# A one-core attention and mixture-of-experts kernel: the second layer norm's inverse deviation is applied to logits and gates instead of to the tokens

## Chip, cores and metric

The kernel runs on one core of a Trainium2 chip. The metric is the device time of one execution in microseconds (us), the median over several runs; lower is better. The engines are TensorE (PE), VectorE (DVE), ScalarE (ACT), GpSimd (POOL) and SyncE (SP, which here only issues transfers).

## What is computed

The input x is 4 images of 64 channels and 1024 positions. The reference, cut to its steps:

```
x = x + wo . softmax_j(k_i . q_j) v            # q, k, v: 32 channels, per image
t = tokens of x                                # 1024 tokens of 64 values per image
t = t + softmax(u u^T) u,      u = layernorm(t)
w = layernorm(t)
logits = w @ router_w + router_b               # 8 experts
top-2 of the softmax over the experts, renormalised: gates
t = t + sum over the 2 chosen experts of gate * (w @ expert_w + expert_b)
```

The last block is the one that the change touches. Layer norm is (t - mean) / sqrt(var + eps), one mean and one variance for each token.

## The kernel before

Every engine has an instruction stream written by hand; streams meet only at semaphores (wait_ge on one side, then_inc on the other). Each image b = 0 to 3 passes through the same stages, and the images are staggered, so that PE works on the first attention of one image, the second attention of the image before it, and the experts of the one before that. T = 8 tiles of 128 tokens make an image.

PE writes most results into a ring of three PSUM buffers of 2 x 512 columns. The list ORDER fixes which use of the ring comes when; use n may start only when use n - 3 has been read (`release` names the semaphore that tells it).

The stages of an image that matter here, with their names:

- `tokens2` (DVE): divides the second attention's output by its row sums (odiv, L1210) and adds the tokens (tok2, L1215).
- `stats_of_2` (DVE): eight BN_STATS, six small operations on 128x8 (L1172 to L1179; the last one signals var2_ready), and cen2 = 8 * (t - mean) (L1180).
- `rstd` (POOL): the inverse deviation, sm2[:, 3, :] = (...)^-0.5 (L372).
- `normalize2` (DVE): wn = cen2 * inverse deviation (L1220), which waits for POOL's L372.
- `w_transposed` (PE, L586): four transposes of wn into the ring ("wT"); `round_w` (ACT, L941) copies them to w_hi, `split_w` (DVE, L1225) makes the rest w_lo.
- `route` (PE, L599): the router's product, high and low weights apart ("rt"); `top2` (DVE, L1233 to L1264): the logits, the two largest of them, and the gates. In the middle of it L1243 makes the gap between the two largest logits, and ACT's `gap_exp` (L945) waits for that gap; ACT runs in order, and the exponentials of an attention stand behind it.
- `experts` (PE, L610): products of w_hi and w_lo with the expert weights, two tiles at a time (g = 0 to 3); `weigh_experts` (DVE, L1275) multiplies them by the gates into prod. POOL sums over experts (L384 to L388, and for the last two images L423), and PE adds what is left in the last two images (L640).
- `copy_agg` (ACT, L925) and `project_out` (PE, L536) end the first attention of an image and feed `tokens1` (DVE, L1156 on); `weigh` (PE, L499) is the product with the probabilities, `copy_att2` (ACT, L929) and `att2_transposed` (PE, L578) end the second attention.

In the last stage DVE's order is: weigh_experts(2, 0), tokens2(3), stats_of_2(3), weigh_experts(2, 1), normalize2(3), weigh_experts(2, 2), split_w(3), weigh_experts(2, 3), top2(3), weigh_experts(3, 0 to 3). POOL's L423 on the products of (2, 1), (2, 2), (2, 3) and (3, 0), (3, 1), (3, 2) runs beside it.

Of the kernel before, what the change touches and what calls it, by code (L numbers as in the profile page):

```python
# [17 lines left out]
ALU = mybir.AluOpType  # L18
# [6 lines left out]
P = 128  # L25
B, C, N, M, E = 4, 64, 1024, 32, 8
CHUNK = 512
T = N // P
# [54 lines left out]
def build(nc, x, wq, wk, wv, wo, rw, rb, ew, eb, out):  # L83
    ctx = ExitStack()
    with ctx:
        def sb(name, shape, dt=F32):
            return ctx.enter_context(nc.sbuf_tensor(name, shape, dt))

        def sem(name):
            return ctx.enter_context(nc.semaphore(name))  # L90

        def two(name, shape, dt=F32):
            return [sb(f"{name}_{n}", shape, dt) for n in range(2)]
# [41 lines left out]
        w_hi = two("w_hi", [P, CHUNK], F32R)  # L135
        w_lo = two("w_lo", [P, CHUNK], F32R)
        gate = two("gate", [P, 2 * T, E])
        ob = two("ob", [P, CHUNK])

        rowmax = sb("rowmax", [P, T])  # L140
# [13 lines left out]
        stats2 = sb("stats2", [P, T, 6])  # L154
        sm2 = sb("sm2", [P, 7, T])
        cen2 = sb("cen2", [P, T, C])
        wn = sb("wn", [P, T, C])
        lg_1 = sb("lg_1", [P, T, E])
        lg = sb("lg", [P, T, E])
        top8 = sb("top8", [P, T, E])  # L160
# [77 lines left out]
        s_ve2 = sem("var2_ready")  # L238
        s_cen2 = sem("centered2_ready")
        s_rs2 = sem("rstd2_ready")  # L240
        s_w = sem("w_ready")
        s_wr = sem("w_rounded")
        s_ws = sem("w_split")
        s_lg1 = sem("logits_first_part")
        s_lg = sem("logits_ready")
        s_top = sem("top2_step")
        s_gap = sem("logit_gap_ready")
        s_eg = sem("gap_exp_ready")
        s_gate = sem("gates_ready")
        s_gT = sem("gates_turned")  # L250
        s_gt = sem("gates_transposed")
        s_gb = sem("expert_bias_summed")
# [21 lines left out]
        def filled(engine, name, b):  # L274
            buf, n = PLACE[(name, b)]
            engine.wait_ge(s_fill, n + 1)
            return ring[:, buf]
# [60 lines left out]
        def _(pool):  # L338
# [77 lines left out]
            rstd(2, s_ve2, s_rs2, sm2)  # L416
            rstd(3, s_ve2, s_rs2, sm2)

            pool.wait_ge(s_w, B)
            for b, pairs in ((2, (1, 2, 3)), (3, (0, 1, 2))):  # L420
                for n, g in enumerate(pairs):
                    pool.wait_ge(s_prod, (T // 2) * b + g + 1)
# [5 lines left out]
        def _(pe):  # L428
            taken = iter(range(len(ORDER)))

            def take(name, b):
                buf, n = PLACE[(name, b)]
                assert n == next(taken), (name, b)
                if n >= RING:
                    pe.wait_ge(*release(*ORDER[n - RING]))
                return ring[:, buf]
# [143 lines left out]

            def w_transposed(b):
                buf = take("wT", b)
                pe.wait_ge(s_w, b + 1)
                w_flat = wn[:, :, :].rearrange("p t c -> p (t c)")
                for g in range(T // 2):
                    mm = pe.transpose(buf[:, 0, g * P:(g + 1) * P], w_flat[:, g * P:(g + 1) * P], ident[:, :])  # L586
                mm.then_inc(s_fill, 1)
# [62 lines left out]
            buf = take("w3", 0)  # L650
# [109 lines left out]
            weigh_pair1(2, 2)  # L760
            scores1(2, 5)
            w_transposed(0)
            scores1(2, 6)
            weigh_pair1(2, 4)
# [40 lines left out]
            weigh_pair1(3, 2)  # L805
            scores1(3, 5)
            w_transposed(1)
            scores1(3, 6)
            weigh_pair1(3, 4)
# [35 lines left out]
            weigh_pair2(3, 2)  # L845
            scores2(3, 5)
            w_transposed(2)
            scores2(3, 6)
            weigh_pair2(3, 4)
# [270 lines left out]
        def _(dve):  # L1120
            def wide(a, n):

                return a.unsqueeze(2).to_broadcast([P, T, n])
# [11 lines left out]
            def row_max(b, tile):  # L1135
                dve.tensor_reduce(rowmax[:, tile:tile + 1], flat(filled(dve, f"mx{tile}", b)), AX.X, ALU.max).then_inc(s_mx, 1)  # L1136
# [49 lines left out]
            def stats_of_2(b):  # L1186
                norm_stats(tok2[b % 2], s_tk2, stats2, sm2, cen2, s_ln2, s_ve2, s_cen2, b)
# [26 lines left out]
                    dve.wait_ge(s_y, b - 1)  # L1214
                dve.tensor_tensor(tok2[b % 2][:, :, :], odiv[:, :, :], tok1[b % 2][:, :, :], ALU.add).then_inc(s_tk2, 1)  # L1215

            def normalize2(b):
                dve.wait_ge(s_cen2, b + 1)
                dve.wait_ge(s_rs2, b + 1)
                dve.tensor_tensor(wn[:, :, :], cen2[:, :, :], wide(sm2[:, 3, :], C), ALU.mult).then_inc(s_w, 1)  # L1220

            def split_w(b):
                buf, _ = PLACE[("wT", b)]
                dve.wait_ge(s_wr, b + 1)
                dve.tensor_tensor(w_lo[b % 2][:, :], ring[:, buf, 0, :], w_hi[b % 2][:, :].bitcast(F32),  # L1225
                                  ALU.subtract).then_inc(s_ws, 1)

            def top2(b):

                buf = filled(dve, "rt", b)  # L1230
                own = gate[b % 2]
                parts = buf[:, 0, 0:2 * T * E].rearrange("p (t a e) -> p t a e", a=2, e=E)
                dve.tensor_tensor(lg_1[:, :, :], parts[:, :, 0, :],  # L1233
                                  rb_all[:, :].unsqueeze(1).to_broadcast([P, T, E]), ALU.add).then_inc(s_lg1, 1)
                dve.wait_ge(s_lg1, b + 1)
                dve.tensor_tensor(lg[:, :, :], parts[:, :, 1, :], lg_1[:, :, :], ALU.add).then_inc(s_lg, 1)
                dve.wait_ge(s_lg, b + 1)
                top = Steps(dve, s_top, 9, b)
                dve.tensor_copy(landing[:, :], lg[:, 0, 0:1])
                for tile in range(T):  # L1240
                    last = dve.max(top8[:, tile, :], lg[:, tile, :])
                top.then(last)
                dve.tensor_tensor(gm[:, 2, :], top8[:, :, 1], top8[:, :, 0], ALU.subtract).then_inc(s_gap, 1)  # L1243

                both = lg[:, :, :].unsqueeze(1).to_broadcast([P, 2, T, E])
                top.then(dve.tensor_tensor(cand[:, :, :, :], both, top8[:, :, 0:2].rearrange("p t n -> p n t").unsqueeze(3)
                                           .to_broadcast([P, 2, T, E]), ALU.is_equal))
                top.then(dve.tensor_tensor(cand[:, :, :, :], cand[:, :, :, :],
                                           ramp[:, :, :].unsqueeze(1).to_broadcast([P, 2, T, E]), ALU.mult))
                top.then(dve.tensor_reduce(gm[:, 0, :], cand[:, 0, :, :], AX.X, ALU.max))  # L1250
                top.then(dve.tensor_tensor(pick1[:, :, :], cand[:, 0, :, :], wide(gm[:, 0, :], E), ALU.is_equal))

                dve.scalar_tensor_tensor(out=cand2[:, :, :], in0=pick1[:, :, :], scalar=-2.0 * E, in1=cand[:, 1, :, :],
                                         op0=ALU.mult, op1=ALU.add)
                dve.wait_ge(s_eg, b + 1)
                top.then(dve.tensor_scalar(gm[:, 4, :], gm[:, 3, :], 1.0, None, ALU.add))
                dve.tensor_reduce(gm[:, 1, :], cand2[:, :, :], AX.X, ALU.max)
                top.then(dve.reciprocal(gm[:, 5, :], gm[:, 4, :]))
                dve.tensor_tensor(pick2[:, :, :], cand2[:, :, :], wide(gm[:, 1, :], E), ALU.is_equal)
                top.then(dve.tensor_tensor(gm[:, 6, :], gm[:, 3, :], gm[:, 5, :], ALU.mult))  # L1260
                dve.tensor_tensor(pick2[:, :, :], pick2[:, :, :], wide(gm[:, 6, :], E), ALU.mult)
                top.then(dve.tensor_tensor(pick1[:, :, :], pick1[:, :, :], wide(gm[:, 5, :], E), ALU.mult))
                top.end()
                dve.tensor_tensor(own[:, 0:T, :], pick1[:, :, :], pick2[:, :, :], ALU.add).then_inc(s_gate, 1)  # L1264

            def weigh_experts(b, g):
                buf = filled(dve, f"e{g}", b)
                if g == 0:
                    dve.wait_ge(s_gate, b + 1)
                if b in (1, 2):  # L1270
                    dve.wait_ge(s_half, (T // 2) * (b - 1) + g + 1)
                if b == 3:
                    dve.wait_ge(s_sums, g + 1)
                gates = gate[b % 2][:, 2 * g:2 * g + 2, :].unsqueeze(3).to_broadcast([P, 2, E, C])
                dve.tensor_tensor(prod[:, g].rearrange("p e h c -> p h e c"), buf.rearrange("p h (e c) -> p h e c", c=C),  # L1275
                                  gates, ALU.mult).then_inc(s_prod, 1)

# [12 lines left out]
            buf = filled(dve, "w3", 0)  # L1290
# [72 lines left out]
            row_max(3, 2)  # L1363
            stats_of_2(0)
            row_max(3, 3)
            normalize2(0)
            split_w(0)
            row_max(3, 4)
            top2(0)
# [14 lines left out]

            tokens2(1)
            stats_of_2(1)
            normalize2(1)
            split_w(1)
            top2(1)

# [8 lines left out]

            tokens2(2)  # L1400
            stats_of_2(2)
            normalize2(2)
            split_w(2)
            top2(2)

# [3 lines left out]
            tokens2(3)  # L1409
            stats_of_2(3)  # L1410
            weigh_experts(2, 1)
            normalize2(3)
            weigh_experts(2, 2)
            split_w(3)
            weigh_experts(2, 3)
# [3 lines left out]
            g = T // 2 - 1  # L1419
# [28 lines left out]
```

## Time and profile before

| | |
|---|---|
| median of 3 runs | 206.97 us (206.75 to 207.73) |
| profiled execution: its own time, its span | 206.87 us, 204.8 us |
| PE busy | 190.6 us (93% of the span) |
| DVE busy | 142.6 us (70%) |
| ACT busy | 108.1 us (53%) |
| POOL busy | 62.9 us (31%) |
| granted TensorE clock | full in all of the span |

Times in the trace count from the start of the span. "Idle before" is how long an engine stood still in front of an instruction, with what ended it. The span is 2.07 us shorter than the time of the same execution, which also has what lies before the first and behind the last recorded instruction.

### The profile page before, as it was taken

How to read it: one execution, taken by the hardware profiler on the slowest of the kernel's cores; microseconds unless marked ns; L12 is line 12 of the kernel's file. 1: busy time of each engine (PE TensorE's matmuls, PEld its weight loads, DVE VectorE, ACT ScalarE, POOL GpSimd, SP SyncE). 2: the span in 40 equal slices, each digit the busy share in tenths (PEclk: the TensorE clock that was granted, in tenths of full speed). 3: DMA queues.
4: the chain of work that ended last, by engine and by line, in shares of the span. 5: the costliest groups of instructions: out<-in, count | busy, mean ns of one | idle time of the engine just before them, and what ended most of it. 6: DMA issues, size and time to landing. Idle time of an engine off the chain costs nothing.

```text
span 204.8 us, 2988 instructions
## 1 busy us (share of the span) xinstructions
PE 190.6 (93%) x1093; PEld 96.8 (47%) x1093; DVE 142.6 (70%) x359; ACT 108.1 (53%) x172; POOL 62.9 (31%) x79
## 2 busy tenths in 40 slices
PE   7989999999999899998989999799999999798993
PEld 2668644464434334543443544253444324386782
DVE  2889666778747894694588865628795361998990
ACT  3765845458845466564376556466563865301010
POOL 8384000003000300012003479700369860026170
PEclk9999999999999999999999999999999999999999
DMA  3890000000000000000000000010000001000022
GB/s 114 200 165 0 3 0 0 2 2 3 0 0 0 3 0 0 0 0 3 0 2 0 3 2 0 18 34 0 3 0 0 3 11 42 0 3 0 0 54 51
DMA packets 3502, 3.69 MB, mean 18 GB/s; under 512 B 2208, under 2 KB 2464, under 8 KB 3488
## 3 DMA queue, kind: packets, MB, share of 16 engines
q1 hardware_dynamic: 3248, 3.45, 7.5%
q8 instruction: 9, 0.15, 0.3%
q10 hardware_dynamic: 240, 0.05, 0.1%
q14 instruction: 5, 0.04, 0.1%
HBM read 2.45 MB, written 1.05 MB: 17 GB/s over the span
## 4 chain that ended last, share of the span: by engine, by line
PE 63%; DVE 23%; POOL 6%; issue 3%; ACT 2%; DMA 1%; SPq 0%; DVEq 0%; POOLq 0%
PE acc L499 20%; PE ring L563 9%; PE ring L474 6%; DVE rowmax L1136 6%; PE ring L492 6%; PE ring L610 3%; POOL sm L372 3%; PE acc L640 2%; PE ring L536 2%; DVE prod L1275 2%; PE ring L547 2%; PE ring L483 2%; DVE stats L1169 2%; PE ring L447 2%; DMA xin<-in_x 1%
## 5 line engine op out<-in xcount | busy, mean ns | idle before, releaser
L372 POOL TENSOR_TENSOR sm<-sm,minus_half 128x8 f32<-128x8 f32 x8 | 15.8, 1974 | 115.8 <-DVE sm L1179 115.8
L920 ACT ACTIVATE prob<-ring,shift 128x1024 f32<-128x1024 f32 x32 | 35.5, 1111 | 23.7 <-PE ring L563 23.3
L1136 DVE TENSOR_REDUCE rowmax<-ring 128x1 f32<-128x1024 f32 x32 | 38.0, 1219 | 12.5 <-PE ring L474 12.4
L917 ACT ACTIVATE prob<-ring 128x1024 f32<-128x1024 f32 x32 | 32.0, 1023 | 19.6 <-PE ring L492 19.5
L499 PE MATMUL acc<-prob,u 128*64 128x512 f32 x128 | 31.2, 606 | 0.4 <-ACT prob L920 0.4
L499 PE MATMUL acc<-prob,val 128*64 128x512 f32 x128 | 31.0, 605 | 0.0
L474 PE MATMUL ring<-qst,kst 96*128 96x512 f32 x64 | 21.9, 429 | 1.2 <-DVE rowmax L1136 0.8
L1275 DVE TENSOR_TENSOR prod<-ring,gate 128x1024 f32<-128x1024 f32 x16 | 19.3, 1220 | 5.1 <-PE ring L610 4.0
L492 PE MATMUL ring<-kst,qst 98*128 98x512 f32 x64 | 21.1, 422 | 0.4 <-DVE rowmax L1136 0.4
L563 PE MATMUL ring<-zsw,zst 64*128 64x512 f16 x64 | 19.4, 376 | 0.0
L563 PE MATMUL ring<-zst,zsw 64*128 64x512 f16 x64 | 19.2, 376 | 0.0
L492 PEld LDWEIGHTS ring<-kst,qst 98*128 98x128 f32 x64 | 10.5, 188 | 11.1 <-ACT prob L917 5.9
L499 PEld LDWEIGHTS acc<-prob,u 128*64 128x64 f32 x128 | 7.7, 136 | 15.9 <-issue 12.5
L499 PEld LDWEIGHTS acc<-prob,val 128*64 128x64 f32 x128 | 7.7, 136 | 15.2 <-issue 12.4
L474 PEld LDWEIGHTS ring<-qst,kst 96*128 96x128 f32 x64 | 10.1, 189 | 9.7 <-DVE rowmax L1136 3.3
L563 PE MATMUL ring<-zst 64*128 64x512 f16 x32 | 12.3, 386 | 0.7 <-DVE rowmax L1136 0.4
L384 POOL TENSOR_TENSOR half<-prod 128x512 f32<-128x512 f32 x8 | 10.6, 1319 | 7.1 <-DVE prod L1275 6.9
L610 PE MATMUL ring<-e,w_hi 64*128 64x512 f32 x64 | 12.4, 443 | 0.0
L563 PE MATMUL ring<-zsw 64*128 64x512 f16 x32 | 12.4, 386 | 0.0
L423 POOL TENSOR_TENSOR prod<-prod 128x512 f32<-128x512 f32 x6 | 7.5, 1279 | 5.8 <-DVE prod L1275 4.9
L563 PEld LDWEIGHTS ring<-zst 64*128 64x128 f16 x32 | 3.0, 93 | 13.3 <-issue 6.5
L1169 DVE BATCH_NORM_STATS2 stats<-tok 128x6 f32<-128x64 f32 x64 | 8.9, 211 | 0.2
(160 smaller groups left out, 319.7 us busy)
## 6 DMA issues: line engine op xcount, KB each, us to landing
xin<-in_x SPq DMA_DIRECT2D x6, 256.0 KB, 5.0
out<-ob SPq DMA_DIRECT2D x6, 128.0 KB, 2.3
xin<-in_x SPq DMA_DIRECT2D x4, 128.0 KB, 2.8
e_in<-in_L_ffn_expert_w SPq DMA_DIRECT2D x2, 128.0 KB
out<-ob SPq DMA_DIRECT2D x4, 64.0 KB, 2.0
eb_in<-in_L_ffn_expert_b SPq DMA_DIRECT2D x8, 2.0 KB
wo<-in_L_conv_wo SPq DMA_DIRECT2D x2, 8.0 KB, 2.2
r_in<-in_L_ffn_router_w SPq DMA_DIRECT2D x2, 2.0 KB
```

The costliest lines, as they stand in the source:

```text
L372: pool.tensor_tensor(sm[:, 3, :], sm[:, 2, :], minus_half[:, :], ALU.pow).then_inc(s_rs, 1)
L384: pool.tensor_tensor(half[:, :, :, :], p[:, 0:E // 2], p[:, E // 2:E], ALU.add).then_inc(s_half, 1)
L474: mm = pe.matmul(buf[:, h, :], kst[home][0:ROW, col(tile):col(tile) + P], qst[home][0:ROW, h * CHUNK:(h + 1) * CHUNK], start=True, stop=True)
L492: mm = pe.matmul(buf[:, h, :], qst[home][0:ROW + 2, col(j):col(j) + P], kst[home][0:ROW + 2, h * CHUNK:(h + 1) * CHUNK], start=True, stop= ...
L499: mm = pe.matmul(acc[h * C:(h + 1) * C, :], stationary[:, j, :], prob[:, j % DEEP, h * CHUNK:(h + 1) * CHUNK], start=(j == 0), stop=(j == ...
L563: mm = pe.matmul(buf[:, h, :], held[h][rows, col(j):col(j) + P], moving[h][rows, h * CHUNK:(h + 1) * CHUNK], start=(n == 0), stop=(n == 2))
L610: mm = pe.matmul(buf[:, h, :], w[rows, g * P:(g + 1) * P], e[rows, :], start=(n == 0), stop=(n == 2))
L917: act.activation(prob1[:, j % DEEP, :], flat(filled(act, f"st{j}", b)), ACT.Exp).then_inc(s_p1, 1)
L920: act.activation(prob2[:, j % DEEP, :], flat(filled(act, f"s{j}", b)), ACT.Exp, bias=shift[:, :], accum_out=rsum2[b % 2][:, j:j + 1]).then ...
L1136: dve.tensor_reduce(rowmax[:, tile:tile + 1], flat(filled(dve, f"mx{tile}", b)), AX.X, ALU.max).then_inc(s_mx, 1)
L1169: last = dve.bn_stats(stats[:, tile, :], tok[:, tile, :])
L1275: dve.tensor_tensor(prod[:, g].rearrange("p e h c -> p h e c"), buf.rearrange("p h (e c) -> p h e c", c=C), gates, ALU.mult).then_inc(s_pr ...
```

## The change

The tokens are no longer multiplied by the inverse deviation. The centred tokens cen2 go through the transposes, the split, the router and the experts; the router's two partial products are multiplied by the inverse deviation when they leave PSUM (lg_2, 128x128, a new instruction, which is also the one that frees the ring buffer "rt"), and a copy of the gates times the inverse deviation (gate_r, 128x64, a new instruction) weighs the experts. The unscaled gates still go to the expert biases.

```
-                dve.tensor_tensor(wn[:, :, :], cen2[:, :, :], wide(sm2[:, 3, :], C), ALU.mult).then_inc(s_w, 1)
...
-            pool.wait_ge(s_w, B)
+            pool.wait_ge(s_cen2, B)
...
-                pe.wait_ge(s_w, b + 1)
-                w_flat = wn[:, :, :].rearrange("p t c -> p (t c)")
+                pe.wait_ge(s_cen2, b + 1)
+                w_flat = cen2[:, :, :].rearrange("p t c -> p (t c)")
...
-                parts = buf[:, 0, 0:2 * T * E].rearrange("p (t a e) -> p t a e", a=2, e=E)
-                dve.tensor_tensor(lg_1[:, :, :], parts[:, :, 0, :],
+                dve.wait_ge(s_rs2, b + 1)
+                dve.tensor_tensor(lg_2[:, :, :, :].rearrange("p t a e -> p t (a e)"),
+                                  buf[:, 0, 0:2 * T * E].rearrange("p (t n) -> p t n", t=T),
+                                  wide(sm2[:, 3, :], 2 * E), ALU.mult).then_inc(s_lg, 1)
+                dve.wait_ge(s_lg, b + 1)
+                dve.tensor_tensor(lg_1[:, :, :], lg_2[:, :, 0, :],
                                   rb_all[:, :].unsqueeze(1).to_broadcast([P, T, E]), ALU.add).then_inc(s_lg1, 1)
-                dve.wait_ge(s_lg1, b + 1)
-                dve.tensor_tensor(lg[:, :, :], parts[:, :, 1, :], lg_1[:, :, :], ALU.add).then_inc(s_lg, 1)
-                dve.wait_ge(s_lg, b + 1)
+                dve.wait_ge(s_lg1, 2 * b + 1)
+                dve.tensor_tensor(lg[:, :, :], lg_2[:, :, 1, :], lg_1[:, :, :], ALU.add).then_inc(s_lg1, 1)
+                dve.wait_ge(s_lg1, 2 * b + 2)
...
                 dve.tensor_tensor(own[:, 0:T, :], pick1[:, :, :], pick2[:, :, :], ALU.add).then_inc(s_gate, 1)
+                dve.wait_ge(s_gate, b + 1)
+                dve.tensor_tensor(gate_r[b % 2][:, :, :], own[:, 0:T, :], wide(sm2[:, 3, :], E), ALU.mult).then_inc(s_gr, 1)
...
                 if g == 0:
-                    dve.wait_ge(s_gate, b + 1)
+                    dve.wait_ge(s_gr, b + 1)
```

Three places show what moves. The first is DVE in the last stage, from the centring of image 3 to the start of its top2; before, it reads:

```order
L1180 SCALAR_TENSOR_TENSOR cen<-tok_1,sm 128x512
L1275 TENSOR_TENSOR prod<-ring,gate 128x2x8x64 [waits prods_used,ring_filled]
L1220 TENSOR_TENSOR wn<-cen,sm 128x512 [waits rstd2_ready,centered2_ready]
L1275 TENSOR_TENSOR prod<-ring,gate 128x2x8x64 [waits prods_used,ring_filled]
L1225 TENSOR_TENSOR w_lo<-ring,w_hi 128x512 [waits w_rounded]
L1275 TENSOR_TENSOR prod<-ring,gate 128x2x8x64 [waits prods_used,ring_filled]
L1233 TENSOR_TENSOR lg<-ring,rb_all 128x64 [waits ring_filled]
L1236 TENSOR_TENSOR lg<-ring,lg 128x64 [waits logits_first_part]
L1239 COPY landing<-lg 128x1 [waits logits_ready]
```

The same place of the changed kernel (its lines are numbered one to four apart from those of before):

```order
L1181 SCALAR_TENSOR_TENSOR cen<-tok_1,sm 128x512
L1277 TENSOR_TENSOR prod<-ring,gate_r 128x2x8x64 [waits prods_used,ring_filled] x2
L1221 TENSOR_TENSOR w_lo<-ring,w_hi 128x512 [waits w_rounded]
L1277 TENSOR_TENSOR prod<-ring,gate_r 128x2x8x64 [waits prods_used,ring_filled]
L1229 TENSOR_TENSOR lg<-ring,sm 128x128 [waits rstd2_ready,ring_filled]
L1233 TENSOR_TENSOR lg<-lg,rb_all 128x64 [waits logits_scaled]
L1236 TENSOR_TENSOR lg<-lg 128x64 [waits logits_step]
L1239 COPY landing<-lg 128x1 [waits logits_step]
```

The wait for POOL's inverse deviation has moved from behind the first product to the start of top2, wn is gone, and the first addition to the logits (L1233) now reads lg_2 in SBUF where it read the ring in PSUM.

The second place is PE in the same stage, where the transposes of image 3 follow the sums over the experts of image 2; before, and then in the changed kernel:

```order
L633 MATMUL acc<-gate_t,eb_blk 128x128 x4
L640 MATMUL acc<-ident,prod 128x128 [waits prods_ready]
L640 MATMUL acc<-ident,prod 128x128 x7
L586 MATMUL ring<-ident,wn 128x128 [waits w_ready,prods_ready]
L586 MATMUL ring<-ident,wn 128x128 x3
L610 MATMUL ring<-e,w_hi 128x512 [waits prods_ready]
```

```order
L634 MATMUL acc<-gate_t,eb_blk 128x128 x4
L641 MATMUL acc<-ident,prod 128x128 [waits prods_ready]
L641 MATMUL acc<-ident,prod 128x128 x7
L587 MATMUL ring<-ident,cen 128x128 [waits centered2_ready,prods_ready]
L587 MATMUL ring<-ident,cen 128x128 x3
L611 MATMUL ring<-e,w_hi 128x512 [waits prods_ready]
```

No PE instruction moves; the transposes wait for the centred tokens instead of the scaled ones, in all four images.

The third place is the end of DVE's top2(2), in the changed kernel:

```order
L1261 TENSOR_TENSOR pick<-pick,gm 128x64 [waits top2_step]
L1262 TENSOR_TENSOR pick<-pick,gm 128x64
L1264 TENSOR_TENSOR gate<-pick 128x64 [waits top2_step]
L1266 TENSOR_TENSOR gate_r<-gate,sm 128x64 [waits gates_ready]
L1406 RECIPROCAL rinv<-rsum_1 128x8 [waits probs2_ready]
L1277 TENSOR_TENSOR prod<-ring,gate_r 128x2x8x64 [waits prods_used,gates_scaled,ring_filled]
```

One instruction, gate_r, has come between the gates and the products; before, the reciprocal (L1407) followed the gates (L1264) directly.

## Rows read from the trace of the kernel before

**Rows 1.** The chain that ended last, share of the span by engine.
```profile
PE 63%; DVE 23%; POOL 6%; issue 3%; ACT 2%; DMA 1%; SPq 0%; DVEq 0%; POOLq 0%
```

**Rows 2.** Waits: engine, line, releaser: us in total, times, longest.
```profile
ACT gm L945 <- DVE gm L1243: 10.3, 4, 3.3
```

**Rows 3.** Timeline of PE, images 0 and 1: start, us, instructions [idle before <-releaser].
```profile
92.78 0.73 PE L492 MATMUL ring<-kst,qst 98*128 98x512 f32 x2
94.15 0.63 PE L586 MATMUL ring<-ident,wn 128*128 128x128 f32 x4 [0.64 <-DVE wn L1220]
...
133.16 0.73 PE L492 MATMUL ring<-kst,qst 98*128 98x512 f32 x2
133.77 0.63 PE L586 MATMUL ring<-ident,wn 128*128 128x128 f32 x4
```

**Rows 4.** Timeline of ACT, PE and DVE around the gap of image 0.
```profile
101.78 0.21 ACT L945 ACTIVATE gm<-gm 128x8 f32<-128x8 f32 x1 [2.94 <-DVE gm L1243]
103.71 0.46 PE L536 MATMUL ring<-wo_blk,agg 128*128 128x130 f32 x2 [0.53 <-ACT agg L925]
104.88 0.21 DVE L1156 RECIPROCAL rinv<-ring 128x8 f32<-128x8 f32 x1 [0.40 <-PE ring L536]
```

**Rows 5.** Timeline of ACT and PE behind the gap of image 1.
```profile
140.90 0.58 ACT L925 ACTIVATE agg<-acc 128x512 f32<-128x512 f32 x1
141.63 1.13 PE L536 MATMUL ring<-wo_blk,agg 128*128 128x130 f32 x8
```

**Rows 6.** Timeline of PE behind the gap of image 2.
```profile
176.86 1.08 PE L499 MATMUL acc<-prob,u 128*64 128x512 f32 x4 [0.40 <-ACT prob L920]
178.63 0.66 PE L578 MATMUL acc<-ident,att 128*128 128x128 f32 x4 [0.70 <-ACT att L929]
```

**Rows 7.** Timeline of DVE, top2 of image 2: small operations.
```profile
174.04 0.22 DVE L1233 TENSOR_TENSOR lg<-ring,rb_all 128x64 f32<-128x64 f32 x1 [1.78 <-PE ring L599]
174.30 0.22 DVE L1236 TENSOR_TENSOR lg<-ring,lg 128x64 f32<-128x64 f32 x1
...
175.39 0.28 DVE L1246 TENSOR_TENSOR cand<-lg,top 128x128 f32<-128x128 f32 x1
```

**Rows 8.** Timeline of all engines, last stage: single rows of it.
```profile
182.76 0.69 DVE L1180 SCALAR_TENSOR_TENSOR cen<-tok,sm 128x512 f32<-128x512 f32 x1
185.89 0.63 PE L586 MATMUL ring<-ident,wn 128*128 128x128 f32 x4 [0.73 <-DVE wn L1220]
187.18 0.69 DVE L1225 TENSOR_TENSOR w_lo<-ring,w_hi 128x512 fp32r<-128x512 f32 x1 [0.31 <-ACT w_hi L941]
187.79 1.21 DVE L1275 TENSOR_TENSOR prod<-ring,gate 128x1024 f32<-128x1024 f32 x1
185.87 2.51 POOL L423 TENSOR_TENSOR prod<-prod 128x512 f32<-128x512 f32 x2 [0.93 <-DVE wn L1220]
189.08 1.29 POOL L423 TENSOR_TENSOR prod<-prod 128x512 f32<-128x512 f32 x1 [0.70 <-DVE prod L1275]
189.17 0.22 DVE L1236 TENSOR_TENSOR lg<-ring,lg 128x64 f32<-128x64 f32 x1
190.16 0.23 DVE L1243 TENSOR_TENSOR gm<-top 128x8 f32<-128x8 f32 x1
194.51 0.73 PE L610 MATMUL ring<-e,w_hi 64*128 64x512 f32 x4
```

**Rows 9.** Timeline, DVE and POOL at once, images 1 and 2.
```profile
128.85 1.28 POOL L397 TENSOR_TENSOR y<-yres,ybias 128x512 f32<-128x512 f32 x1
128.91 1.24 DVE L1173 SCALAR_TENSOR_TENSOR sm<-stats 128x8 f32<-128x8 f32 x1
...
163.30 0.69 DVE L1215 TENSOR_TENSOR tok<-odiv,tok 128x512 f32<-128x512 f32 x1
163.38 1.74 POOL L397 TENSOR_TENSOR y<-yres,ybias 128x512 f32<-128x512 f32 x1
...
165.26 0.17 DVE L1173 SCALAR_TENSOR_TENSOR sm<-stats 128x8 f32<-128x8 f32 x1
```

More of the change, by code:

```diff
@@ L137, in build @@
         gate = two("gate", [P, 2 * T, E])
+        gate_r = two("gate_r", [P, T, E])
         ob = two("ob", [P, CHUNK])
@@ L156, in build @@
         cen2 = sb("cen2", [P, T, C])
-        wn = sb("wn", [P, T, C])
+        lg_2 = sb("lg_2", [P, T, 2, E])
         lg_1 = sb("lg_1", [P, T, E])
@@ L240, in build @@
         s_rs2 = sem("rstd2_ready")
-        s_w = sem("w_ready")
         s_wr = sem("w_rounded")
         s_ws = sem("w_split")
-        s_lg1 = sem("logits_first_part")
-        s_lg = sem("logits_ready")
+        s_lg = sem("logits_scaled")
+        s_lg1 = sem("logits_step")
         s_top = sem("top2_step")
@@ L249, in build @@
         s_gate = sem("gates_ready")
+        s_gr = sem("gates_scaled")
         s_gT = sem("gates_turned")
@@ L1215, in tokens2 @@
                 dve.tensor_tensor(tok2[b % 2][:, :, :], odiv[:, :, :], tok1[b % 2][:, :, :], ALU.add).then_inc(s_tk2, 1)
-            def normalize2(b):
-                dve.wait_ge(s_cen2, b + 1)
-                dve.wait_ge(s_rs2, b + 1)
-                dve.tensor_tensor(wn[:, :, :], cen2[:, :, :], wide(sm2[:, 3, :], C), ALU.mult).then_inc(s_w, 1)
             def split_w(b):
@@ L1273, in weigh_experts @@
                     dve.wait_ge(s_sums, g + 1)
-                gates = gate[b % 2][:, 2 * g:2 * g + 2, :].unsqueeze(3).to_broadcast([P, 2, E, C])
+                gates = gate_r[b % 2][:, 2 * g:2 * g + 2, :].unsqueeze(3).to_broadcast([P, 2, E, C])
                 dve.tensor_tensor(prod[:, g].rearrange("p e h c -> p h e c"), buf.rearrange("p h (e c) -> p h e c", c=C),
@@ L1365, in _ @@
             row_max(3, 3)
-            normalize2(0)
             split_w(0)
@@ L1386, in _ @@
             stats_of_2(1)
-            normalize2(1)
             split_w(1)
@@ L1401, in _ @@
             stats_of_2(2)
-            normalize2(2)
             split_w(2)
@@ L1411, in _ @@
             weigh_experts(2, 1)
-            normalize2(3)
             weigh_experts(2, 2)
```

## The prediction, written before the changed kernel ran

> **What bounds the kernel now.** The first view is the chain that ended last, by engine: PE holds 63% of the span, DVE 23%, POOL 6% [rows 1]. So a DVE instruction counts only where the chain leaves PE. The view of waits shows where that may be. ACT stands 10.3 us in all in front of `gap_exp`, once per image, for DVE's gap of the logits [rows 2]. The timeline then has three kinds of place. At the transposes of wn, PE stands still 0.64 us in image 0 and 0.73 us in image 3, both times for wn, which itself has waited for POOL's inverse deviation; in image 1 the transposes follow without a stop [rows 3, 8], and in image 2 too. Behind the gap of image 0 ACT goes on with an exponential and the copy agg, and PE waits 0.53 us for agg [rows 4]; in image 1 agg ends at 140.90 + 0.58 = 141.48 and PE's L536 starts at 141.63, just behind it [rows 5]; in image 2 PE waits 0.40 and 0.70 us for ACT [rows 6]. Last, from the third product of image 2 to the last stage's end, DVE's top2(3) leads: the experts' product of (3, 3) on PE starts at 194.51, when DVE's first product of image 3 has freed the ring [rows 8].
>
> **The change, part by part.** *New lg_2.* It is 128x128, PSUM times SBUF. The nearest rows: 0.22 us for 128x64 from PSUM, 0.28 for 128x128 from SBUF, and a dependent instruction starts 0.26 after the one of 0.22 [rows 7]. I take 0.28 and a step of 0.32 us; bounds 0.26 (no cost for the second 64 columns) and 0.35. It stands before the gap, so every gap is 0.32 later than it would be. *New gate_r.* 128x64, 0.22 us, a step of 0.26. It stands behind the gap; in images 0 and 1 DVE then waits for PE anyway (0.40 us before L1156 in image 0 [rows 4]), and in image 2 the PE path below covers it. In image 3 nothing hides it. *Gone: wn*, 0.69 us on DVE, and the wait for POOL in front of it.
>
> *Image 0.* PE no longer waits. In image 1, with no wait, the transposes start 133.77 - 133.16 = 0.61 us behind the product before them; here 94.15 - 92.78 = 1.37. The difference is 0.76, a little more than the idle time shown, since loading the first weights also hides. cen2 has been ready since before L492 here. Copy w_hi, w_lo, route and the next maximum follow 0.75 earlier, the gap 0.75 - 0.32 = 0.43 earlier, and agg, L536 and everything behind them as well: **-0.43 us** (-0.32 if only the idle time of 0.64 is saved).
>
> *Image 1.* No wait for wn to save, and the gap comes 0.32 later. agg is what PE waits for, with nothing to spare: **+0.32 us**. It goes on into tokens1(3), which waits for L536.
>
> *Image 2.* The gap is 0.32 later, so the last exponential, PE's L499 at 176.86 and the transposes at 178.63 are: +0.32 on PE. DVE is 0.58 later (lg_2 and gate_r) when it comes to tokens2(3), so cen2 of image 3 ends at 182.76 + 0.69 + 0.58 = 184.03. PE would be free for the transposes at about 185.16 + 0.32 = 185.48 (185.89 less the idle 0.73, later by the gap), so PE sets their start, not DVE. They start 0.73 - 0.32 = 0.41 us earlier than before by the idle time alone, and 0.52 if the first weights hide as in image 0 (0.11 more). I take **-0.52** for them, and so for w_hi, w_lo and the product of (2, 3), which wait for each other in a row. POOL's inverse deviation was there before the transposes of wn at 185.89; 0.58 later it is still in time for top2(3), which starts behind the product of (2, 3) at 187.79 [rows 8].
>
> *Top2(3).* Here an addition changes its kind. L1233 read PSUM and SBUF; now it reads lg_2 and rb_all, both in SBUF, while POOL's L423 works on the product of (2, 3). Rows 9 show what that means: DVE's L1173 on 8 columns, both inputs in SBUF, takes 0.17 us at 165.26 with POOL idle, and 1.24 at 128.91, begun 0.06 after POOL's L397, ending at 130.15 where POOL ends at 130.13. The other way round, DVE's L1215 began 0.08 before L397, took its usual 0.69, and POOL's took 1.74 instead of 1.28 [rows 9]. An operation with one input in PSUM is not held: L1225 takes 0.69 in the middle of two L423 [rows 8]. L1243 at 190.16 (both inputs in SBUF) ends at 190.39, POOL's L423 at 190.37 [rows 8]. So who comes first holds the other off until it ends. Before, POOL starts 189.08 - 187.79 = 1.29 us behind the start of the product, and L1236 at 1.38. The new L1233 stands where L1236 stood plus the 64 columns of lg_2, at 1.45, which is 0.16 after POOL; POOL ends at 2.58. The addition ends at about 2.65 (64 columns at 1.05 ns, from L1225's 0.69 for 512 against 0.22 for 64), not at 1.67: **+0.98 us**, bounds 0 (it comes first) and 1.2 (it comes right behind and runs in full). Against that, L1243 isn't held any more: 0.23 against the 0.17 of such an operation, -0.06. With lg_2 0.32 and gate_r 0.26, top2(3) gives +0.98 - 0.06 + 0.58 = +1.50, less the 0.52 saved: **+0.98** at the first product of image 3. PE waits for that product, and POOL, DVE and PE keep their distances to the end.
>
> The Trainium skill, "SBUF — State Buffer", the section on the single rule of port contention, says that a VectorE instruction with two SBUF inputs and a GpSimd instruction that reads SBUF exclude each other for a whole instruction, and that the issue order decides who blocks. By that rule the trace agrees, at each place named; by a model without it the sum would be near -0.1.
>
> *The sum:* -0.43 + 0.32 + 0.98 = +0.87 against the profiled execution's 206.87, which stands 0.10 under the median of 206.97; the difference is laid on the median: 207.8. Savings by idle time alone and a late hold give +1.1; the longest hidden weights and a step of 0.26 for lg_2 give +0.6. So 207.5 to 208.1 if the addition is held.
>
> **The rivals.** *The addition isn't held.* It needs POOL to start 0.16 us later, or DVE earlier. For it: the lead of 0.16 is small, and worked out from three durations. Against: 0.06 was enough at 128.91 [rows 9]. Then the sum is -0.43 + 0.32 + 0.58 - 0.06 - 0.52 = -0.11: 206.9.
>
> *Faster: ACT's wait for the gap has slack.* If exponentials behind `gap_exp` were not on the path, lg_2 would cost nothing in images 1 and 2, and image 0 would keep its 0.75. Then 206.97 - 0.75 - 0.84 (0.52 + 0.32 at the transposes of image 3) + 0.52 (top2(3), not held) = 205.9; with the hold 206.9. It decides from 0.32 us of slack between agg and L536. The rows speak against it: in all three images PE waits for ACT or starts 0.15 behind it [rows 4, 5, 6].
>
> *More slower: image 0's gain doesn't arrive.* Something else than wn (the exponential that frees the ring, w_hi queued behind an exponential on ACT) would hold the route. Then 0.75 comes on top: 207.84 + 0.75 = 208.6. Against it: in image 1 the transposes had nothing to wait for, and PE has no idle time before its route or the product behind it.
>
> *The change doesn't act.* PE's order is the same, only the semaphore differs, and the centring really ends before PE is free in images 0 and 3; this one I leave at nothing.
>
> **Chances.** Held addition, as forecast: 0.67. Not held: 0.15. Slack at the gap: 0.06. Gain lost: 0.12. A measurement of this kernel tells about 0.5%, 1.03 us, from no change. The forecast's sum is 0.4%, with about a quarter of its weight above 0.5%: slower 0.17 + 0.12 + 0.03 = 0.32; faster 0.06; same 0.62. The range takes in the not held case below and most of the lost gain above: 206.7 to 208.5.
>
> **What would show it.** Held: in the changed profile the addition to lg_2 in image 3 takes about 1.2 us and ends where L423 on the product of (2, 3) ends, and 0.22 in images 0 to 2. PE's idle time before the transposes of cen2 is gone in images 0 and 3, there 0.41 to 0.52 us earlier against L578 of the second attention moved by 0.32. The distance from the transposes to L536 in image 0 is 0.32 longer, in image 1 L536 has an idle time of about 0.3 for agg. The prediction is wrong if the hold is missing, if L536 in image 1 isn't later against y's transposes, or if the time of the tail behind the first product of image 3 changes.

## The result and the profile after

| | before | after |
|---|---|---|
| median of 20 runs | 206.94 us | 207.68 us |
| span of the profiled execution | 204.8 us | 205.4 us |
| PE, DVE, ACT, POOL busy | 190.6, 142.6, 108.1, 62.9 us | 190.1, 142.9, 108.0, 62.9 us |

The ratio is 1.003, with a 95% interval of 1.0021 to 1.0038: the change costs 0.3%, some 0.6 to 0.7 us, clear of the noise and under the 0.5% that the prediction took as the least difference to be told. The forecast was 207.8. One of the 20 runs of the kernel before (215.15 us) and five of the 20 of the changed kernel (210.6 to 210.9 us, at a mean granted clock of 0.984) fell in a slower state, and such runs are left out of this ratio and all below.

The chain that ended last, share of the span by engine; it is [rows 1] with three points of DVE gone and two more on ACT:

```profile
PE 64%; DVE 20%; POOL 6%; ACT 4%; issue 3%; DMA 1%; SPq 0%; DVEq 0%; POOLq 0%
```

The view of waits has the same row as [rows 2], larger by 2.3 us:

```profile
ACT gm L946 <- DVE gm L1243: 12.6, 4, 4.5
```

Image 0 and image 1 in the timeline of PE and ACT of the changed kernel (start, us, instructions, [idle before <-releaser]):

```profile
92.70 0.73 PE L493 MATMUL ring<-kst,qst 98*128 98x512 f32 x2
93.26 0.60 PE L587 MATMUL ring<-ident,cen 128*128 128x128 f32 x4
...
101.18 0.21 ACT L946 ACTIVATE gm<-gm 128x8 f32<-128x8 f32 x1 [3.27 <-DVE gm L1243]
103.12 1.13 PE L537 MATMUL ring<-wo_blk,agg 128*128 128x130 f32 x8 [0.86 <-ACT agg L926]
...
139.38 0.21 ACT L946 ACTIVATE gm<-gm 128x8 f32<-128x8 f32 x1 [1.57 <-DVE gm L1243]
141.31 1.13 PE L537 MATMUL ring<-wo_blk,agg 128*128 128x130 f32 x8 [0.39 <-ACT agg L926]
```

Against [rows 3] the transposes of image 0 follow the product before them after 0.56 us instead of 1.37. Against [rows 4] the gap and L537 (L536 before) come 0.60 and 0.59 earlier, and PE's wait for agg has grown from 0.53 to 0.86: of what PE gained, 0.33 is given back at the gap. Against [rows 5] L537 of image 1 is only 0.32 earlier, with a wait of 0.39 that wasn't there. (All of this execution runs 0.09 us earlier from the first row maximum on, before any changed instruction; that 0.09 is not the change's.)

Behind the gap of image 2, against [rows 6], the same once more, 0.40 grown to 0.73:

```profile
176.90 1.08 PE L500 MATMUL acc<-prob,u 128*64 128x512 f32 x4 [0.73 <-ACT prob L921]
178.68 0.66 PE L579 MATMUL acc<-ident,att 128*128 128x128 f32 x4 [0.70 <-ACT att L930]
```

The last stage, DVE, POOL and PE, against [rows 8]:

```profile
185.02 0.60 PE L587 MATMUL ring<-ident,cen 128*128 128x128 f32 x4
186.29 0.69 DVE L1221 TENSOR_TENSOR w_lo<-ring,w_hi 128x512 fp32r<-128x512 f32 x1 [0.28 <-ACT w_hi L942]
186.90 1.21 DVE L1277 TENSOR_TENSOR prod<-ring,gate_r 128x1024 f32<-128x1024 f32 x1
188.03 0.28 DVE L1229 TENSOR_TENSOR lg<-ring,sm 128x128 f32<-128x128 f32 x1
188.19 1.29 POOL L424 TENSOR_TENSOR prod<-prod 128x512 f32<-128x512 f32 x1 [0.36 <-DVE prod L1277]
188.34 1.21 DVE L1233 TENSOR_TENSOR lg<-lg,rb_all 128x64 f32<-128x64 f32 x1
189.59 0.23 DVE L1236 TENSOR_TENSOR lg<-lg 128x64 f32<-128x64 f32 x1
190.59 0.17 DVE L1243 TENSOR_TENSOR gm<-top 128x8 f32<-128x8 f32 x1
...
193.65 0.30 PE L620 MATMUL acc<-ident,gate 128*128 128x128 f32 x1 [1.72 <-DVE gate L1264]
193.85 2.36 DVE L1277 TENSOR_TENSOR prod<-ring,gate_r 128x1024 f32<-128x1024 f32 x2
195.13 0.73 PE L611 MATMUL ring<-e,w_hi 64*128 64x512 f32 x4 [0.29 <-DVE prod L1277]
```

The first product of image 3 (DVE), where the account below ends, in the kernel before:

```profile
193.23 3.49 DVE L1275 TENSOR_TENSOR prod<-ring,gate 128x1024 f32<-128x1024 f32 x3
```

Up to the product at 186.90 DVE is 0.89 earlier than before (187.79). L1233, an addition over 64 columns, then takes 1.21 us; it begins 0.15 behind POOL's L424 and ends at 189.55, 0.07 behind POOL's end at 189.48. In images 0 to 2, where POOL does nothing meanwhile, the same instruction takes 0.22 to 0.23. DVE's first product of image 3 starts at 193.85 instead of 193.23, and PE's L611 behind it at 195.13 instead of 194.51: the lead of 0.89 has become a lag of 0.62.

### The profile page after: what moved, and what is told of

It reads as the page before. It is cut to its first block, busy times and chain, and to the rows that moved or that the text cites. A ratio compares the mean times of both kernels' runs of the same rounds, so it can differ in the third digit from the quotient of the medians.

```text
span 205.4 us, 2992 instructions
## 1 busy us (share of the span) xinstructions
PE 190.1 (93%) x1093; PEld 96.9 (47%) x1093; DVE 142.9 (70%) x363; ACT 108.0 (53%) x172; POOL 62.9 (31%) x79
## 4 chain that ended last, share of the span: by engine, by line
PE 64%; DVE 20%; POOL 6%; ACT 4%; issue 3%; DMA 1%; SPq 0%; DVEq 0%; POOLq 0%
PE acc L500 21%; PE ring L564 8%; PE ring L493 7%; PE ring L475 6%; DVE rowmax L1137 5%; PE ring L611 3%; PE acc L641 3%; PE ring L537 2%; DVE prod L1277 2%; PE ring L548 2%; POOL half L385 2%; ACT prob L921 2%; PE ring L448 1%; DMA xin<-in_x 1%; PE acc L465 1%
## 5 line engine op out<-in xcount | busy, mean ns | idle before, releaser
L1277 DVE TENSOR_TENSOR prod<-ring,gate_r 128x1024 f32<-128x1024 f32 x16 | 19.2, 1220 | 5.1 <-PE ring L611 4.0
L611 PE MATMUL ring<-e,w_hi 64*128 64x512 f32 x64 | 12.4, 443 | 0.3 <-DVE prod L1277 0.3
L1221 DVE TENSOR_TENSOR w_lo<-ring,w_hi 128x512 fp32r<-128x512 f32 x4 | 2.8, 692 | 11.7 <-ACT w_hi L942 11.7
L424 POOL TENSOR_TENSOR prod<-prod 128x512 f32<-128x512 f32 x6 | 7.5, 1275 | 6.1 <-DVE prod L1277 6.0
```

What stands on the lines that cost most here:

```text
L424: pool.tensor_tensor(prod[:, g, 0:E // 2], prod[:, g, 0:E // 2], prod[:, g, E // 2:E], ALU.add).then_inc(s_half, 1)
L611: mm = pe.matmul(buf[:, h, :], w[rows, g * P:(g + 1) * P], e[rows, :], start=(n == 0), stop=(n == 2))
```

## The experiments

The theory is that of the prediction: four terms, of which the largest is a hold of 1 us on one addition, because DVE's instruction with two inputs in SBUF and POOL's sum exclude each other. Its rivals: two more instructions on DVE are enough to explain the tail; the gap is not what PE waits for; the gain of image 0 is lost later. Ratios stand against runs of the kernel before on the same chip, with 95% intervals. Each edit moves the line numbers by a few; the operands say which instruction it is. Several kernels are compared below on one distance, which leaves out all that happened earlier: from PE's transposes of the second attention of image 3 (L578 of the kernel before) to DVE's first product of image 3.

### lg_2 written to PSUM

```
-                dve.tensor_tensor(lg_2[:, :, :, :].rearrange("p t a e -> p t (a e)"),
-                                  buf[:, 0, 0:2 * T * E].rearrange("p (t n) -> p t n", t=T),
+                scaled = buf[:, 0, 0:2 * T * E].rearrange("p (t n) -> p t n", t=T)
+                dve.tensor_tensor(scaled, scaled,
                                   wide(sm2[:, 3, :], 2 * E), ALU.mult).then_inc(s_lg, 1)
...
-                     "wT": (s_ws, b + 1), "rt": (s_lg, b + 1), "yT": (s_ob, b + 1)}
+                     "wT": (s_ws, b + 1), "rt": (s_lg1, 2 * b + 2), "yT": (s_ob, b + 1)}
```

> The changed kernel with lg_2 written back in place into the ring buffer in PSUM instead of into SBUF, so that both additions to the logits read one operand from PSUM again; the ring buffer is freed by the second addition. Theory (the addition is held off by the sum on POOL): L1233 of image 3 takes 0.22 us instead of 1.21, nothing else moves, and the time falls by 1.0 us from 207.7 to 206.7, 0.2 to 0.4 under the kernel before. Rival (the tail is longer because of the two more DVE instructions, and the long addition is only where DVE waits for something else): 207.6, with the idle time somewhere else in top2(3).

Measured: 206.60 us, ratio 0.9983 (0.9974 to 0.9993). DVE and POOL in its last stage:

```profile
188.27 1.30 POOL L423 TENSOR_TENSOR prod<-prod 128x512 f32<-128x512 f32 x1 [0.37 <-DVE prod L1277]
...
188.11 0.29 DVE L1230 TENSOR_TENSOR ring<-ring,sm 128x128 f32<-128x128 f32 x1
188.44 0.22 DVE L1233 TENSOR_TENSOR lg<-ring,rb_all 128x64 f32<-128x64 f32 x1
188.69 0.22 DVE L1236 TENSOR_TENSOR lg<-ring,lg 128x64 f32<-128x64 f32 x1
```

The same addition begins 0.17 behind the same POOL operation, with one input in PSUM, and is not held. The instructions on DVE are as many as in the changed kernel, so their number does not explain this 1 us. The distance is 192.96 - 178.75 = 14.21 us, against 193.85 - 178.68 = 15.17 in the changed kernel: the hold costs 0.96.

### POOL's sum made short

```
+                    rows = slice(0, 1) if (b, g) == (2, 3) else slice(0, E // 2)
+                    other = slice(E // 2, E // 2 + 1) if (b, g) == (2, 3) else slice(E // 2, E)
+                    cols = slice(0, 8) if (b, g) == (2, 3) else slice(0, C)
-                    pool.tensor_tensor(prod[:, g, 0:E // 2], prod[:, g, 0:E // 2], prod[:, g, E // 2:E],
+                    pool.tensor_tensor(prod[:, g, rows, :, cols], prod[:, g, rows, :, cols], prod[:, g, other, :, cols],
```

> The changed kernel with DVE untouched, but POOL's sum on the product of (2, 3) cut from 128x512 to 128x16, so it leaves out most of that sum. Theory: the POOL operation is over, or nearly, when L1233 of image 3 comes; that addition takes 0.22 to 0.35 us, and the time falls by 0.85 to 1.0 us, to 206.7 to 206.9. Rival (POOL is not the cause): L1233 still takes 1.2 us and the time stays at 207.6.

Measured: 206.49 us, ratio 0.9977 (0.9967 to 0.9988), 0.2 under the lowest that was expected. DVE's program is that of the changed kernel word for word, and the addition is short:

```profile
188.15 0.22 POOL L427 TENSOR_TENSOR prod<-prod 128x16 f32<-128x16 f32 x1 [0.36 <-DVE prod L1280]
...
188.30 0.23 DVE L1236 TENSOR_TENSOR lg<-lg,rb_all 128x64 f32<-128x64 f32 x1
```

POOL's part in it is shown from the other side: 192.82 - 178.63 = 14.19 us on the same distance, so the hold costs 0.98 by this kernel.

### POOL's sum started later

```
+                    if (b, g) == (2, 3):
+                        pool.wait_ge(s_lg1, 2 * B - 1)
```

> The changed kernel with POOL's sum on the product of (2, 3) waiting also for the first addition to the logits of image 3. Theory (who comes first holds the other off, each time anew): L1233 takes 0.22, L1236 comes first as well or is held from its first moment, and if it comes first then POOL starts behind it at about 188.83 and ends at about 190.1, where L1243 (both inputs in SBUF, due at 189.59) ends too: a hold of about 0.5 instead of 1.0, time 207.2. If POOL comes before L1236 the whole hold of 1.2 lies on L1236 instead and the time stays at 207.7. Rival (a hold only ever falls on the first addition): 206.7.

Measured: 206.87 us, ratio 0.9991 (0.998 to 1.0002), lower than the 207.2 of the theory and nearer to the rival's 206.7, so the time alone doesn't decide. The timeline does:

```profile
188.38 0.23 DVE L1235 TENSOR_TENSOR lg<-lg,rb_all 128x64 f32<-128x64 f32 x1
188.64 0.23 DVE L1238 TENSOR_TENSOR lg<-lg 128x64 f32<-128x64 f32 x1
188.75 1.30 POOL L426 TENSOR_TENSOR prod<-prod 128x512 f32<-128x512 f32 x1 [0.88 <-DVE lg L1235]
...
189.64 0.43 DVE L1245 TENSOR_TENSOR gm<-top 128x8 f32<-128x8 f32 x1
190.00 0.28 DVE L1248 TENSOR_TENSOR cand<-lg,top 128x128 f32<-128x128 f32 x1
```

The hold moves on, as the theory says: both additions are free, and the next instruction with two inputs in SBUF, the gap, takes 0.43 instead of 0.17 and ends at 190.07, POOL's sum at 190.05. Its cost is 14.45 us on the distance above, less the 14.20 of the two kernels without a hold: 0.25, not 0.5. The expectation counted the hold from the start of the gap; unheld, the gap would have ended at 189.64 + 0.17 = 189.81, and it ended 0.26 after that. POOL began at 188.75, inside the second addition, and took its usual 1.30 (more on this in the last section).

### lg_2 alone, on the kernel before

```
+                dve.tensor_tensor(lg_2[:, :, :, :].rearrange("p t a e -> p t (a e)"),
+                                  buf[:, 0, 0:2 * T * E].rearrange("p (t n) -> p t n", t=T),
+                                  wide(unit[:, :], 2 * E), ALU.mult).then_inc(s_lg2, 1)
+                dve.wait_ge(s_lg2, b + 1)
-                dve.tensor_tensor(lg_1[:, :, :], parts[:, :, 0, :],
+                dve.tensor_tensor(lg_1[:, :, :], lg_2[:, :, 0, :],
```

> The kernel before with lg_2 alone: the router's products are multiplied by a tile of ones on their way from PSUM to SBUF; wn stays, the gates stay. Theory: +0.33 at the gap of image 0, +0.33 at that of image 1, +0.32 on DVE's way through top2(2) to the centring of image 3, and in top2(3) 0.32 plus a hold of 1.0 less 0.06: +2.2 us in all, 209.15. Rival without a hold: +1.3 us, 208.2. Rival in which the gap has slack: +1.5 us, from top2(2) and top2(3) alone, 208.5.

Measured: 209.20 us, ratio 1.0103 (1.0087 to 1.0119), +2.2. The addition of image 3 takes 1.22 us here too. The start of L536 in image 0 is 0.33 later than before (104.04 against 103.71), in image 1 it is 142.32 against 141.63, another 0.36.

### gate_r alone, on the kernel before

```
+                dve.wait_ge(s_gate, b + 1)
+                dve.tensor_tensor(gate_r[b % 2][:, :, :], own[:, 0:T, :], wide(unit[:, :], E), ALU.mult).then_inc(s_gr, 1)
```

> The kernel before with gate_r alone: the gates are multiplied by a tile of ones into a copy, and the copy weighs the experts. Theory: hidden in images 0 and 1, where DVE then waits for L536; 0.26 in image 2, because before the change DVE and POOL, not PE, set the start of image 3's transposes; 0.26 in image 3: +0.52, 207.45. Rival (hidden in image 2 as well): 207.2. Rival (on the path in all four): 208.0.

Measured: 207.41 us, ratio 1.0027 (1.0015 to 1.0038), +0.56. PE's L536 in images 0 and 1 and the transposes of the second attention of image 3 (178.66, 178.63 before) are where they were; the w transposes of image 3 are 0.28 later (186.17), the first product of image 3 is 0.55 later (193.78). In the changed kernel the first 0.28 is hidden: there PE has no idle time before these transposes, so PE and not DVE sets their start.

### The change in image 0 alone, and in image 3 alone

In both, an image that goes the old way has wn again and neither lg_2 nor gate_r:

```
+                if b in OLD:
+                    pe.wait_ge(s_w, OLD.index(b) + 1)
+                else:
+                    pe.wait_ge(s_cen2, b + 1)
+                w_flat = (wn if b in OLD else cen2)[:, :, :].rearrange("p t c -> p (t c)")
```

> The change in image 0 alone; images 1 to 3 go the old way. Theory: the 0.5 us by which L536 of image 0 came earlier in the changed kernel stay to the end, nothing else differs: 206.4. Rival (the start of image 0's gain is lost again by image 1, and the saving comes from image 3): 206.9.

Measured: 206.51 us, ratio 0.9977 (0.9965 to 0.9989), -0.48. L541 (the L536 of before) of image 0 starts at 103.07, 0.64 earlier than before, and what is behind it keeps this to within 0.03: the first product of image 3 is at 192.62, against 193.23. Of the 0.61 that are left, 0.11 lie before the change's first instruction. The gain of image 0 arrives at the end.

> The change in image 3 alone, with lg_2 in SBUF as in the changed kernel (the ring buffer is freed by the second addition); images 0 to 2 go the old way. Theory: the transposes start 0.9 earlier, top2(3) takes 1.5 more with the hold: +0.57, 207.5. Rival (the saving at the transposes and the cost of the hold cancel): 206.9.

Measured: 207.40 us, ratio 1.0026 (1.0016 to 1.0036), +0.54. The gain and the hold in one view:

```profile
186.91 1.22 DVE L1293 TENSOR_TENSOR prod<-ring,gate 128x1024 f32<-128x1024 f32 x1
...
188.20 1.28 POOL L428 TENSOR_TENSOR prod<-prod 128x512 f32<-128x512 f32 x1 [0.63 <-DVE prod L1293]
188.36 1.21 DVE L1248 TENSOR_TENSOR lg<-lg,rb_all 128x64 f32<-128x64 f32 x1
```

The product is 0.88 earlier than before; the first product of image 3, at 193.86, is 0.63 later. (Here the second addition frees the ring buffer, so PE waits 0.62 us for it at 189.88; that costs nothing at the first product of image 3, which starts 15.18 us behind the transposes at 178.68, against 15.17 in the changed kernel.)

### The change in images 0 and 3, lg_2 in PSUM

OLD is (1, 2) here, and lg_2 stays in the ring as in the first experiment.

> lg_2 in PSUM as in the first experiment, and the change made only in images 0 and 3, where the transposes waited for wn; images 1 and 2 go the old way (wn, no lg_2, no gate_r). Theory: image 0 keeps its gain of 0.5, images 1 and 2 lose nothing (the gap comes 0.33 earlier than in the first experiment in both), image 3 has the 0.92 of the transposes less 0.58 for lg_2 and gate_r and nothing held: 0.95 under the kernel before, 206.0. Rival (the 0.33 of the gap is hidden in images 1 and 2): as the first experiment, 206.6.

The same kernel once more, for its profile:

> The kernel of the old way in images 1 and 2 once more, for a profile of an undisturbed execution. Theory: the gap of image 1 comes 9.4 us behind the transposes of y (9.4 before the change, 9.7 with it), L536 of image 1 follows its predecessor without idle time, image 2 likewise; 206.0 to 206.2.

Measured: 206.24 and then 205.96 us, ratios 0.9962 (0.9948 to 0.9975) and 0.9954 (0.9941 to 0.9966). The gap of image 1 comes 139.22 - 129.80 = 9.42 us behind the transposes of y, and L540 of image 1 has no idle time before it; both as expected. It is 0.2 to 0.3% under the first experiment, which differs only in images 1 and 2: lg_2 costs there, and there is little or nothing to gain.

### The exponential of the gap later in ACT's order

```
-            gap_exp(0)
...
             exp2(1, 0)
             copy_agg(2)
+            gap_exp(0)
```

and so in images 1 and 2 (there it comes behind the last exponential). First on the kernel with the old way in images 1 and 2:

> The kernel of the old way in images 1 and 2, and ACT's order changed: the exponential of the gap comes behind the exponential and the copy agg (images 0 and 1) and behind the last exponential (image 2), so that neither waits for DVE's gap. Theory (PE waits at L536 and at the last L499 only because ACT waits for the gap): L536 of image 0 follows without idle time, of which the next work on DVE lets 0.65 through; 0.13 in image 1; 0.6 in image 2 at w_lo of image 3; together 1.4 less than without it: 204.6 (204.3 to 205.0). Rival (DVE's top2 sets the pace by itself): less than 0.3 gained, 205.8.

Measured: 205.22 us, ratio 0.9919 (0.9906 to 0.9933), the lowest of all, but above the range expected (204.3 to 205.0): it gained 0.7 to 1.0 us of the 1.4. Then with the change in all four images and lg_2 in PSUM:

> The first experiment (the change in all images, lg_2 in PSUM) with ACT's exponential of the gap behind the exponential and the copy agg. If the gap costs its 0.33 in images 1 and 2 only because ACT waits for it, this comes within 0.3 us of the kernel that has the same order of ACT and the old way in those images (205.2): 205.3 to 205.6. If the gap's lateness costs on DVE too, 205.9 or more.

Measured: 205.64 us, ratio 0.9937 (0.9924 to 0.9951), just above what was expected. PE's waits in this kernel between the w transposes of image 0 and those of image 3, without one of 0.18:

```profile
106.94 0.39 PE L563 MATMUL ring<-zst 64*128 64x512 f16 x1 [0.71 <-DVE rowmax L1134]
129.47 0.63 PE L572 MATMUL ring<-ident,y 128*128 128x128 f32 x4 [1.26 <-POOL y L397]
151.68 1.05 PE L547 MATMUL ring<-ident_h,uhl 128*128 128x128 f16 x16 [0.54 <-DVE uhl L1195]
177.20 0.66 PE L578 MATMUL acc<-ident,att 128*128 128x128 f32 x4 [0.70 <-ACT att L929]
```

The last three are in the changed kernel too (1.28, 0.49 and 0.70). The waits for agg (0.86 and 0.39) and for the last exponential (0.73) are gone, so they were the gap's. A new one of 0.71 has come in image 0, for a row maximum that stands behind top2 on DVE; the kernel of 205.22 has it too. It shows why that kernel missed its range. Without the new order its L540 of image 0 (the L536 of before) starts 103.24 - 86.01 = 17.23 us behind the second attention's transposes before it, with it 102.28 - 86.07 = 16.21, so 1.02 is won; at the next transposes of that kind only 0.23 of it are left (38.70 against 38.93 behind the same ones), where 0.65 was expected. In image 1 nothing was won, where 0.13 was expected, and image 2 gave 0.63, as expected.

Last, that order of ACT on the kernel before:

> The kernel before with that order of ACT alone. Theory: 0.6 in image 0 and 0.13 in image 1; nothing in image 2, where DVE and POOL set the start of image 3's transposes: 206.2. Rival (DVE's top2 sets the pace by itself): 206.9.

Measured: 206.53 us, ratio 0.9999 (0.9978 to 1.0021); no difference is shown. Its ten runs fall apart by the granted clock: six at 0.997 or more take 206.25 to 206.57 us (their median is 206.36, not far above the 206.2 expected), three at 0.991 take 207.1 to 207.3, and one at 0.983 takes 208.62. The profiled execution is one of those at 0.991. In it the last stage reaches the transposes 0.55 earlier than before, and then this (view of windows: us, busy time and instructions of PE, PEld, DVE, ACT, POOL, granted clock, share of the DMA engines, GB/s):

```profile
183.00:185.30 2.30, 0.98 (x9) 0.79 (x8) 1.84 (x3) 0.00 (x0) 1.40 (x1) 1.00 0.00 0
...
186.50:188.00 1.50, 1.50 (x12) 1.14 (x8) 1.36 (x2) 0.10 (x1) 1.34 (x2) 0.86 0.00 0
188.00:190.00 2.00, 2.00 (x10) 1.64 (x11) 1.90 (x14) 0.12 (x1) 1.28 (x1) 0.50 0.00 0
190.00:191.00 1.00, 1.00 (x8) 0.73 (x6) 0.86 (x5) 0.09 (x1) 0.00 (x0) 0.50 0.00 0
```

The granted clock is at the lower of its two levels, 1.2 GHz, from about 187.6 (0.86 is the mean over a stretch of 1.5 us) to 191, and the end comes 0.2 later than before. So the order of ACT seems to gain some 0.5 us, and the lower clock takes it back in four runs of ten; the 17 runs of the kernel before beside them have no clock under 0.997. This split was made after the runs, and what makes the clock fall was not tried.

## Why the prediction was right

Term by term, in us, each measured in the profiled execution of the changed kernel against that of before. A place's shift is the difference of its two start times; a term is how far the shift changes from one place to the next.

| term | forecast | shift at its end | measured |
|---|---|---|---|
| before the change's first instruction | 0 | -0.09 | -0.09 |
| image 0: transposes without wait, gap later | -0.43 | -0.59 (L537) | -0.50 |
| image 1: gap later | +0.32 | -0.32 (L537) | +0.27 |
| up to route of image 2 | 0 | -0.29 | +0.03 |
| image 2: gap later | +0.32 | +0.05 (L579) | +0.34 |
| transposes of image 3 against L579, to the product of (2, 3) | -0.84 | -0.89 (DVE L1277) | -0.94 |
| top2(3): hold, lg_2, gate_r | +1.50 | +0.62 (L1277) | +1.51 |
| sum | +0.87 | | +0.62, or +0.71 without the first row |

Behind the first product of image 3 nothing changes, as the forecast said: the span ends 11.57 us after it before, and 11.55 after. The forecast was right by its terms and not by errors that cancel: leaving out the first row, three terms missed by 0.05 to 0.10, all towards a faster kernel, and the others by 0.03 or less.

**The hold.** The forecast was 0.98, and it cost 0.96 or 0.98 (first and second experiment), with the place, POOL's lead (0.16 forecast, 0.15 in the profile) and the end as forecast. Four kernels show its cause: it goes when the addition reads PSUM, it goes when POOL's sum is short, it moves to the gap when POOL comes later, and it appears on the kernel before when lg_2 is put in SBUF. The Trainium skill's "SBUF — State Buffer", under "Who interferes with whom", names this case, two SBUF inputs against a GpSimd instruction that reads SBUF. Its rule that the issue order decides who blocks agrees with the changed kernel, where POOL was first and DVE held for 0.99 us, and with DVE's side of the third experiment, where DVE was first and not held. The three rivals that the forecast priced are out: the addition is held; lg_2 alone cost 0.33 and 0.36 in images 0 and 1, so the gap has no slack; and with the change in image 0 alone its gain of 0.50 is there at the end.

**lg_2 and gate_r.** 0.28 us and a step of 0.32; 0.22 and a step of 0.26, as taken from the rows. gate_r was hidden in images 0 and 1 and, in the changed kernel, in image 2.

**Image 0 and the transposes of image 3.** Both gains were sized from PE's idle time, with 0.11 added for weights that load under the product before. They were 0.50 instead of 0.43 and 0.94 instead of 0.84, so the term that was mis-sized is this one, by 0.07 and 0.10. The row that the first was measured by, image 1 in [rows 3], was itself not free of wn: without wn the transposes follow the product before them after 0.56 or 0.57 us instead of 0.61, and the product behind them after 0.35 instead of 0.39. The whole gain of image 0 at that product is 0.83 (0.91 earlier, at 93.62 against 94.53, less 0.08 from before), where the forecast had 0.75.

**Image 1.** +0.27 instead of +0.32, for the same reason: the product before the transposes is 0.57 earlier than before, the one behind them 0.65 (133.51 against 134.16). The profile of before showed no idle time there, but wn ended at 132.93 + 0.69 = 133.62 and the transposes started 0.15 later. That is the distance at which they follow wn in image 0 too, where PE did wait for it (93.31 + 0.69 = 94.00, then 94.15). The forecast had put the saving of image 1 at nothing; it was 0.08, and the gap then cost its 0.33.

What the whole comes to: PE gains 0.83, 0.08 and 0.94 us at the transposes of images 0, 1 and 3; three gaps, 0.33 later each, take 1.0 of it back, and top2(3) costs 1.5. With lg_2 kept in PSUM the change is a gain of 0.2% (first experiment), and with the change made in images 0 and 3 alone as well, one of 0.4 to 0.5%.

## What to carry to other kernels

Moving a multiplication to a smaller tensor is priced by where the new instruction stands, not by its columns: here 128 columns in front of a value that another engine waits for cost 0.33 us in each of three images, and the 512 columns taken away had been waited for in two. Look at which memory each operand of a moved or new DVE instruction comes from, and at what POOL does at that moment; keeping one operand in PSUM was worth 1 us. And make a change image by image: it pays where the profile shows the wait that it removes, and costs where it doesn't.

## What was not expected of the hardware

The second DVE addition of the third experiment ran from 188.64 to 188.87 with both inputs in SBUF, and POOL's sum, which began at 188.75, took its usual 1.30 us. By the rule of "SBUF — State Buffer" in the Trainium skill, that the one that starts first has the ports for its whole instruction and the other fully blocks, POOL would have been blocked for the 0.12 that was left, and the trace shows 1.30 against 1.29. Five other places, where POOL's instruction begins inside a DVE instruction with two SBUF inputs, show how much that is worth: in [rows 9] DVE's L1215 had 0.61 left, and POOL took 0.46 longer than the 1.28 at 128.85; in the changed kernel 0.47, 0.45, 0.46 and 0.60 were left (POOL's instructions at 126.60, 149.05, 151.60 and 163.10), and POOL took 0.33, 0.30, 0.32 and 0.46 longer than the same instruction elsewhere. In all five POOL loses 0.14 to 0.15 less than what DVE has left when POOL's record begins, so by these rows the 0.12 of the third experiment costs nothing. Where the 0.15 comes from was not tried.

With the exponential of the gap moved on the kernel before, PE stood still 1.36 us before the transposes of image 3, and 2.2 us after it went on the granted clock fell to half, until 191; the product of 4 x 512 columns at 188.19 took 1.22 us instead of 0.73. In the profiled execution of the changed kernel an idle time of 1.72 us before L620 was followed by no fall. Whether the five runs of the changed kernel with a mean clock of 0.984 fell there, no trace shows.
